# Graph attention on one core: one transfer per ScalarE issue, a larger ScalarE share of the row sums, a new order of TensorE's opening work, and SyncE's branch ahead of its wait for stores

## The reference

```python
s_i = emb @ attn[:d];  s_j = emb @ attn[d:]          # emb is x
e = leaky_relu(s_i + s_j.T, negative_slope=0.2)
e = e + where(adj > 0, 0, -1e9)
alpha = softmax(e, axis=1)
out = layernorm(x + alpha @ emb, axis=-1)
```

## Time and profile before

| | |
|---|---|
| median of 3 runs | 263.21 us (263.14 to 263.3) |
| the profiled execution's own time | 262.65 us |
| its span | 260.8 us |
| TensorE matmul busy | 247.6 us (95%) |
| VectorE busy | 236.0 us (90%) |
| ScalarE busy | 165.8 us (64%) |
| chain of work that ended last | 86% in the products of line 801 |

### The profile page before, as it was taken

The page is one execution under the profiler, slowest core; times in us unless marked ns, Lnnn a source line. Parts: engine busy times, 40 slices in busy tenths (PEclk is TensorE's granted clock), DMA queues, the critical chain, the costliest instruction groups (busy, mean ns, idle before and its releaser), DMA issues.

```text
span 260.8 us, 5350 instructions
## 1 busy us (share of the span) xinstructions
PE 247.6 (95%) x2117; PEld 240.9 (92%) x2117; DVE 236.0 (90%) x385; ACT 165.8 (64%) x241; POOL 36.7 (14%) x74
## 2 busy tenths in 40 slices
PE   7968899999999999999999999999999999999970
PEld 6646899999999999999999999999999999999970
DVE  1949999999999999999999999999999999999261
ACT  1349989986875798539971797359832995054010
POOL 1000000000330033003300330015000330033022
PEclk9999999999999999999999999999999999999996
DMA  6999999999999999999999999999999930001001
GB/s 198 319 348 348 349 349 347 350 349 348 349 349 359 350 349 356 355 349 348 347 362 349 336 284 363 341 343 285 364 342 343 265 110 0 3 0 44 0 0 43
DMA packets 70236, 71.67 MB, mean 275 GB/s; under 512 B 2881, under 2 KB 68674, under 8 KB 70210
## 3 DMA queue, kind: packets, MB, share of 16 engines
q10 hardware_dynamic: 34592, 34.67, 42.9%
q1 hardware_dynamic: 34594, 34.67, 42.8%
q0 software_dynamic: 1024, 1.97, 2.3%
HBM read 69.21 MB, written 2.10 MB: 273 GB/s over the span
## 4 chain that ended last, share of the span: by engine, by line
PE 90%; DVE 3%; ACT 2%; ACTq 1%; POOL 1%; issue 1%; POOLq 0%; DVEq 0%
PE psum L801 86%; DVE weights L669 1%; ACTq L249 1%; PE psum L754 1%; PE psum L780 1%; PE psum L769 1%; DVE mask_bytes L578 1%; ACT adj_in L345 1%; POOL out_dram L257 1%; DVE mask_t L573 1%; ACT adj_in L352 0%; ACT x_raw L456 0%; PE psum L757 0%; PE psum L759 0%; DVE x_raw L614 0%
## 5 line engine op out<-in xcount | busy, mean ns | idle before, releaser
L801 PEld LDWEIGHTS psum<-xj,weights 128*128 128x128 f32 x2048 | 229.0, 192 | 2.8 <-issue 2.8
L801 PE MATMUL psum<-xj,weights 128*128 128x129 f32 x2048 | 229.3, 275 | 1.8 <-issue 0.9
L669 DVE SCALAR_TENSOR_TENSOR weights<-q_row,r_j,mask_t 128x512 f32<-128x512 f32 x256 | 172.7, 739 | 1.8
L385 ACT ACTIVATE mask_bytes<-adj_in 128x4096 uint8<-128x4096 int32 x27 | 96.9, 3607 | 15.4 <-DMA adj_in<-in_adj_dram 15.4
L560 DVE STREAM_TRANSPOSE mask_t<-mask_bytes 128x1024 uint32<-128x1024 uint32 x27 | 33.4, 1235 | 0.0
L391 ACT ACTIVATE x_raw<-x_raw 128x128 f32<-128x128 f32 x28 | 8.3, 298 | 36.1 <-DVE x_raw L614 35.8
L309 POOL TENSOR_SCALAR neg_mean<-total 128x4 f32<-128x4 f32 x7 | 3.7, 525 | 170.2 <-ACT x_raw L391 170.2
L318 POOL DMA_DIRECT2D out_dram<-x_raw x28 | 14.6, 527 | 20.5 <-ACT x_raw L405 20.4
L379 ACT ACTIVATE mask_bytes<-adj_in 128x2048 uint8<-128x2048 int32 x8 | 15.1, 1897 | 0.0
L398 ACT ACTIVATE unused<-x_raw,neg_mean 128x128 f32<-128x128 f32 x28 | 10.9, 390 | 4.6 <-POOL neg_mean L309 4.6
L405 ACT ACTIVATE x_raw<-x_raw,offset,rstd 128x128 f32<-128x128 f32 x28 | 11.5, 480 | 2.3 <-POOL offset L315 2.3
(11 more groups left out here) (58 smaller groups left out, 59.6 us busy)
## 6 DMA issues: line engine op xcount, KB each, us to landing
adj_in<-in_adj_dram ACTq DMA_DIRECT2D x64, 512.0 KB, 14.7
adj_in<-in_adj_dram SPq DMA_DIRECT2D x64, 512.0 KB, 13.9
out_dram<-x_raw POOLq DMA_DIRECT2D x28, 64.0 KB, 5.3
x_raw<-in_x_dram ACTq DMA_DIRECT2D x4, 128.0 KB, 3.1
x_raw<-in_x_dram SPq DMA_DIRECT2D x4, 128.0 KB, 3.7
x_raw<-in_x_dram ACTq DMA_DIRECT2D x2, 256.0 KB, 6.1
x_raw<-in_x_dram SPq DMA_DIRECT2D x2, 256.0 KB, 6.7
out_dram<-x_raw POOLq DMA_DIRECT2D x4, 32.0 KB, 1.9
```

Of the source, the lines that this page charges most:

```text
L385: nc.scalar.activation(mask_bytes[:, g % BYTE_SLOTS, :, :, :], adj_in[:, g % ADJ_SLOTS, :, :, :], ACT.Sign).then_inc(bytes_ready, 1)
L669: nc.vector.scalar_tensor_tensor(weights[:, slot_of(n, c), :], q_row[:, n * BANK:(n + 1) * BANK], r_j[:, c:c + 1], mask_t[:, (n * PIECES + ...
L801: return nc.tensor.matmul(banks[(n * K + t) % 8][:, 0:D1], weights[:, slot_of(n, c), t * P:(t + 1) * P], xj[:, c, 0:D1], start=(c == 0), s ...
```

## The change

Four edits. ScalarE sums all eight chunks of stripe 2, VectorE none of them. ScalarE issues its transfers singly and at other places: in the opening those of piece 2 come after the sums and after the last copy; in the loop quadrant 3 is issued for piece g+2 and quadrant 2 for piece g+3. TensorE does all turns and `s_i_piece` 0 to 3 ahead of the spreading of the maxima, and pieces 4 to 7 behind it. SyncE waits for the last stores behind its branch.

```diff
-    S_J_BY_ACT = slice(2 * SC, 2 * SC + K)
+    S_J_BY_ACT = 2
@@ SyncE, at the end
-            sp.wait_ge(last_stored, 16 * Q * (len(FINAL_GROUPS) - EARLY))
             sp.wait_ge(again_ready, 1)
             with sp.If(sp.value_load(again[0:1, 0:1], min_val=0, max_val=1) > 0):
                 sp.wait_ge(stored, 16 * Q * NORM_GROUPS)
                 sp.wait_ge(early_stored, 16 * Q * EARLY)
+                sp.wait_ge(last_stored, 16 * Q * (len(FINAL_GROUPS) - EARLY))
...
+            sp.wait_ge(last_stored, 16 * Q * (len(FINAL_GROUPS) - EARLY))
@@ ScalarE, the copies of the turned x
-                if m < 4:
-                    load_piece(act, HIGH_HALF[m % 2:m % 2 + 1], 1 + m // 2)
-                if m == K:
-
-                    act.wait_ge(products_ready, 3)
-                    for c in range(S_J_BY_ACT.start, S_J_BY_ACT.stop):
+                if m == 0:
+                    load_piece(act, HIGH_HALF[0:1], 1)
+                if m == 2:
+                    load_piece(act, HIGH_HALF[1:2], 1)
+                if m == 4:
+
+                    act.wait_ge(products_ready, S_J_BY_ACT + 1)
+                    for c in range(S_J_BY_ACT * SC, (S_J_BY_ACT + 1) * SC):
                         last = nc.scalar.activation(prod[:, c, :], prod[:, c, :], ACT.Identity, accum_out=s_j[:, c:c + 1])
                     last.then_inc(s_j_by_act_ready, 1)
+                    load_piece(act, HIGH_HALF[0:1], 2)
+            load_piece(act, HIGH_HALF[1:2], 2)
@@ ScalarE, before and in the loop over the pieces
             q_piece(0)
-            load_piece(act, HIGH_HALF[0:1], 3)
             act.wait_ge(factors_ready, 1)
             scale_xj(0, 1)
             q_piece(1)
-            load_piece(act, HIGH_HALF[1:2], 3)
             q_piece(2)
             q_piece(3)
+            load_piece(act, HIGH_HALF[0:1], 3)
             scale_xj(1, PC)
+            load_piece(act, HIGH_HALF[1:2], 3)
             for g in range(BY_DVE, ALL_PIECES):
                 bytes_may_go(g)
                 if g in HALVED:
                     half_to_bytes(g, 0)
-                    load_piece(act, HIGH_HALF, g + IN_FLIGHT)
+                    if g > BY_DVE:
+                        load_piece(act, HIGH_HALF[1:2], g + 2)
                     if g < PIECES:
                         scale_xj(g * PC, g * PC + K)
                     half_to_bytes(g, 1)
+                    load_piece(act, HIGH_HALF[0:1], g + 3)
...
                 else:
                     to_bytes(g)
-                    if g + IN_FLIGHT < ALL_PIECES:
-                        load_piece(act, HIGH_HALF, g + IN_FLIGHT)
+                    if g + 2 < ALL_PIECES:
+                        load_piece(act, HIGH_HALF[1:2], g + 2)
+                    if g + 3 < ALL_PIECES:
+                        load_piece(act, HIGH_HALF[0:1], g + 3)
@@ VectorE, the sums
-            sum_products(3, stripe(3))
-            sum_products(2, slice(S_J_BY_ACT.stop, 3 * SC))
-
-            dve.wait_ge(s_j_ready, STRIPES)
+            sum_products(3)
+
+            dve.wait_ge(s_j_ready, STRIPES - 1)
@@ TensorE, the opening
-            turn_x(0)
-            for m in range(1, 4):
+            for m in range(4):
                 turn_x(m)
-                s_i_piece(m - 1)
+            s_i_piece(0)
+            s_i_piece(1)
             turn_x(4)
+            turn_x(5)
+            s_i_piece(2)
+            turn_x(6)
+            turn_x(7)
             pe.wait_ge(attn_j_ready, 1)
             s_i_piece(3)
-            for m in range(5, RB):
-                turn_x(m)
-            s_i_piece(4)
             pe.wait_ge(row_max_ready, 1)
             pe.wait_ge(xT_ready, MAX_BANK + 1)
             nc.tensor.matmul(banks[MAX_BANK][:, 0:P], smax[:, 0:1].broadcast_to([P, P]), ident[:],
                              start=True, stop=True).then_inc(max_spread, 1)
-            for rb in range(5, RB):
+            for rb in range(4, RB):
                 s_i_piece(rb)
```

More of the change, by code:

```diff
@@ L508, in _, with sum_products @@
         def _(dve):
-            def sum_products(st, c):
+            def sum_products(st):
+                c = slice(st * SC, (st + 1) * SC)
                 dve.wait_ge(products_ready, st + 1)
                 nc.vector.reduce_sum(s_j[:, c], prod[:, c, :], X).then_inc(s_j_ready, 1)
-            def stripe(st):
-                return slice(st * SC, (st + 1) * SC)
             def product_of(st):
@@ L530, in _ @@
             product_of(0)
-            sum_products(0, stripe(0))
+            sum_products(0)
             dve.wait_ge(x_loaded[1], 16 * Q)
             product_of(1)
-            sum_products(1, stripe(1))
+            sum_products(1)
             dve.wait_ge(x_loaded[2], 16 * Q)
```

## The result

The changed kernel takes 260.19 us (259.07 to 260.58, 4 runs) against 263.17 us (262.93 to 263.3, 4 runs): ratio 0.9887, interval 0.9865 to 0.9909, 3.0 us less. Measured twice more, it takes 259.24 us against 262.76 (ratio 0.986, 0.9838 to 0.9882) and 259.25 against 262.82 (0.9859, 0.9831 to 0.9887): 3.5 and 3.6 us less. The forecast was 260.7, range 260.3 to 262.2. The sign and the mechanism (the landing of piece 0 as what VectorE waits for) were right, and the gain was larger than the 2.5 us that I called the most there could be.

A forecast was written before the change was run, and what follows sets the result against it. TensorE's unbroken products were taken as the bound, so only their start could move: 2.5 us off the 260.8 us span gives 258.3, a profiled 260.15 and a median of 263.21 - 2.5 = 260.7 us. Range 260.3 to 262.2.

The forecast's parts named there:

- Piece 0 is late next: Opening: VectorE's bytes wait for SyncE's second transfer of piece 0, landing at 17.1 us, so they start at 17.15.
- the most that the opening can give: Start of VectorE's bytes moving from 19.68 to 17.15: at most 2.53 us gained, taken as 2.5.
- What bounds the kernel: TensorE's products, one unbroken piece of 223.76 us from 27.32; only their start, later hold-ups and what follows count.
- ScalarE's sums and the row maximum: Opening: eight sums end near 15.55, row maximum done near 15.8 instead of 17.46, 1.66 us earlier.
- The spreading: TensorE's spreading of the maxima takes 0.7 us, bounded by 0.24 and 1.10, ending at 16.5 instead of 19.12.
- s_i pieces 4 to 7: TensorE between spreading and products: 3.66 us, covered, with 1.0 us of cover ahead of the fifth tile.
- Unblocking in the loop is worth nothing by itself: ScalarE's transfer issues in the loop: no gain, since TensorE has no pause behind 27.32; worth something only as slack.
- Piece 1's 0.17 us to spare: Piece 1 lands at 23.1, its bytes are ready at 25.05, and VectorE wants them at 25.22.
- TensorE's order: Turns and s_i pieces 0 to 3 end at 15.8, so TensorE reaches its wait when the maximum comes.
- SyncE's branch: End of program: moving 0.9 us of loading and branching is worth 0, at most 0.2 us.
- The loads did not set the pace: Rival 4 (a): loads set the pace, a piece every 7.8 us against TensorE's 7.16, giving 277 us; chance 0.04.
- rival 4 (b): Clock falls at the wait for the maxima: pieces 4 to 7 take 7.3 us, 3.7 us later, 266.9; chance 0.04.

The follow-up runs named there:

- experiment 10: The kernel before with only SyncE's branch put ahead of its wait for stores: 262.71 us, ratio 0.9996.
- experiment 1: The changed kernel measured once more, no edit, for its spread and a second profile: 259.24 us.
- experiment 3: The changed kernel with quadrant 0 of piece 1 ahead of quadrant 1 of piece 0 on SyncE: 262.57 us, against 259.25 for the unedited changed kernel.
- experiment 7: The kernel before with only ScalarE's transfers at their new places in the opening and the loop: 260.19 us against 262.76, ratio 0.9891.
- experiment 8: The changed kernel with TensorE's order of before: 261.13 us, ratio 0.9918 to the kernel before.
- the control: The changed kernel, unedited, measured beside a version with four sums back on VectorE: 259.25 us, ratio 0.9859 to the kernel before.
- experiment 5: The changed kernel with ScalarE's transfers of the loop, piece 3's two among them, at their old places: 262.95 us, ratio 0.9988 to the kernel before.
- experiment 4: The changed kernel with piece 0's bytes made from x instead of adj, without the wait for its landing: 259.67 us, ratio 0.9869 to the kernel before.
- experiment 6: The changed kernel with ScalarE's transfers of the opening at their old places: 262.98 us, ratio 1.0007 to the kernel before.

## Why the prediction was wrong

The step that failed is the one headed "Piece 0 is late next". It took the landing of one execution, 17.1 us, for a fixed point, and with it 2.53 us for "the most that the opening can give". The step was the right one: in the changed kernel VectorE's bytes start on that landing in every profile. But in the twelve profiles in which SyncE issued this transfer as before, it landed at 16.4 to 17.2 us: 17.1 and 16.8 in the kernel before and in experiment 10, 16.4, 16.5 and 17.0 in the three of the changed kernel, and 16.6 to 17.2 in the other seven, with the old and the new places of ScalarE's transfers alike; and the start of the kernel before is itself a draw (19.68 and 20.06). The difference of the two is 2.5 to 3.6, with a middle near 3.1. I had the pessimistic ends of both and gave the range too little room on the fast side, 0.4 us. In the two profiles the sum comes out: the 2.53 us of the prediction, 0.72 for bytes at 16.43 instead of 17.15, and 0.25 behind the products make the 3.5 us of the span. The measured 260.19 is 0.11 us below the range, 259.24 and 259.25 are 1.1 below. So the mechanism held, and the term that was mis-sized is the landing. How far below the range the median came was a matter of draws as well: the profiled execution after, 259.07, is the fastest of the four on record, and the other three took 259.83 to 260.58.

Point by point:

- What bounds the kernel, the 7.64 us from the bytes to the products, and the unbroken 223.76 us: right. In the profiles of experiments 1, 3, 7, 8 and of the control the distance is 7.63 to 7.65.
- ScalarE's sums and the row maximum, forecast done near 15.8: it starts at 14.31 to 15.25. I had counted the fifth turn's end at 12.4 with TensorE slow as in the profile before; in the profile after TensorE was fast and the copy came at 11.19. In the control it was slow (16 turning passes in 3.67 us from 5.85) and the row maximum at 15.25, where the forecast had it start near 15.6: still 0.35 early. s_i pieces 0 to 3, which I had ended at 15.8, were done at 14.18 in the profile after and at 15.21 in the control, so TensorE waited for the maximum. The landing covered all of this.
- The spreading, 0.7 us from the row maximum's end to the next reduction: 0.58. Right within the bounds.
- Piece 0's landing: the mis-sized term, above. It was put at 17.1, and measured 16.4 to 17.2.
- s_i pieces 4 to 7, 3.66 us, covered: 3.62, and TensorE still idled 0.89 us ahead of the fifth tile. Right.
- "Unblocking in the loop is worth nothing by itself": right as put, as no pause existed behind 27.32 before. But the size of what hangs on it was missed. I looked for slack at the pieces' landings and not at the issues of piece 3, which would have been in the way of `q_row`. With the loop's and piece 3's issues at their old places nothing measurable is left of the gain (experiment 5).
- Piece 1's 0.17 us to spare: in the profile after its last transfer landed at 22.4, its first half was there at 24.38 and VectorE took it at 24.51 without waiting. The margin was right, and partly by luck: piece 1 had been taken to land at 23.1 and landed 0.7 us earlier, just as VectorE wanted it 0.7 us earlier. Experiment 4, where it landed at 23.0, shows it as the next bound.
- TensorE's order was counted with the spreading and not by itself: without it 1.0 to 1.6 us are lost by the profiles, 1.9 by the medians (experiment 8).
- SyncE's branch, 0: right (experiment 10).
- The rivals: the clock did not fall at the wait for the maxima. The granted clock is full in every slice of the page after but the last, and the s_i pairs behind the spreading took 3.62 / 4 = 0.91 us. TensorE had been idle 0.36 us. The Trainium skill, "TensorE: Matmul & The Clock Gate", the section on how the clock oscillates in real kernels, would have had the clock fall at an idle gap. Behind these 0.36 us it did not. Behind the 3.63 us of experiment 6 it did, with granted clock 0.50 and 5.32 us for the four pieces, and there the trace agrees with the page; rival 4 (b) had priced this at 7.3 us for the pieces and 3.7 us in all, and it cost about 0.1, since the clock came back after some 3 us and the pause ahead of the fifth tile took up the rest. The loads did not set the pace either: ScalarE's transfers took 13.4 us in the median from issue to landing, before 14.7.

No kernel tried here is faster than the changed one.

## What to carry to other kernels

A transfer's issue is free only where its queue has room or where its engine has other work queued, and whether it has depends on the time at which the issue comes. When the work around it moves earlier, look up each issue again, on the engine that issues and on those that wait for what stands behind it: here either half of ScalarE's transfers, put back to its old places, took the whole gain away (experiments 5 and 6), and one of the halves had been priced at nothing.

Where a transfer becomes the bound, one execution gives one draw of its landing. Take it from several, and give the range room on both sides.

## What the runs showed of the hardware

- The landing of the same transfer, issued at 4.7 us behind the same loads, spread over 0.8 us (16.4 to 17.2) from execution to execution.
- An issue of 512 KB on ScalarE took 0.59 us at best. Held, single ones took 1.4 to 3.2 us in the rows above, and ScalarE stood idle for up to 2.34 us of it. The number of transfers still under way does not settle which: in the changed kernel the issue at 12.48 took 0.59 us and the one at 13.37 took 1.83 us, each with four earlier ones of ScalarE's queue not yet landed.
- TensorE's granted clock fell to 0.50 for some 3 us in two profiles: behind 3.63 us of idle time (experiment 6), and behind 1.16 and 1.55 us with four short passes between them (experiment 5). Behind 2.16 us in the kernel before it stayed full, and so it did behind 2.74 us in the profile of experiment 3, so the length of the last idle stretch alone does not settle it.
- TensorE's passes in the opening are slow or fast from one execution to the next: eight turning passes from 5.4 us took 1.09 us in two profiles of the changed kernel, sixteen from 5.85 took 3.67 us in the third, and eight from 5.86 took 1.97 before, while the granted clock of the page is full in all four.
